# Two passages between stages and the start: where constants, first weights, the last turn and attention's rings stand

## The chip, the cores and the metric

One core of one Trainium2 chip runs the whole program. The metric is the device time of one execution, in microseconds (us). The core has five engines: TensorE (PE) for products, VectorE (DVE), ScalarE (ACT), GpSimd (POOL), and SyncE (SP), which here only issues transfers. Each runs its own list of instructions in order and waits on semaphores for the others.

## What is computed

Two layers on x of shape (4, 512, 512), in float32. Layer 0 attends from x to a context of 1601 rows per batch and gates the result; layer 1 is a transformer block whose products use one of two weight sets per token (`vm`). Cut to what the change touches:

```
memory_proj = memory @ W_mem.T                      # layer 0
attn = softmax(x @ memory_proj.T / sqrt(512))
memory_context = attn @ memory_proj
gate = sigmoid(concat([x, memory_context]) @ W_gate.T + b_gate)
x = rmsnorm(x + gate * memory_context, norm_w)

vm = (tt[:, :-1] == 1) & (tt[:, 1:] == 1)           # layer 1; the last token is False
mixed = where(vm, rmsnorm(x) @ v_qkv, rmsnorm(x) @ l_qkv)
q, k, v = split(mixed); q, k = rotary(q), rotary(k) # 16 heads of 32, tables by position_ids
x = x + where(vm, ctx @ v_dense, ctx @ l_dense)     # ctx = causal softmax(q k) v
... cross attention to the encoder rows, then a gated feed-forward, also by vm
```

## The kernel before, in words

The program is a row of stages, each a function with its own semaphores. A stage ends in `clear` (L71): a barrier of all engines, POOL clears the stage's semaphores, a second barrier. Within a stage each engine's list is written out by hand. The change touches the first three stages and the few lines that call them.

Nearly every product of two float32 operands is made of three (`three`, L106 to L108): each operand is split into a high part, a rounded copy, and a low part, the rest. The split of a weight tile, 128 x 512, loaded to the ring `w_raw` of 4, is a cast (high) and a subtraction (low).

**First stage, `gated_context` (L111).** A turn for each of the 4 batches. PE computes the maxima of rough scores (L443) in turn with the gate's share of x; DVE reduces them and makes `shift`; then come 13 key tiles, each with scores on PE, exponential on ACT (L251), a running sum on POOL and values on PE (L483). After the last tile DVE copies the values (L389), PE sums the columns (L524), DVE inverts (L391), PE spreads the inverse (L531), and the gate's second share follows. Between these short steps PE runs the four pieces of the next batch's first projection (`project`, L420), except in the last batch, where there is no next. The stream of batch b stays in `h` and is stored to `fused_d` by SP (L199, the last one L205).

Ahead of the first batch: SP loads x, W_mem, the context, the second half of W_gate and weight tiles, while ACT issues eight transfers of constants (L232, L236). DVE turns positions into a one-hot tile `hot`, which lies in `h`, copies masks and identities, then splits W_mem; PE multiplies the one-hot tile by the table (L490), which gives `cos_t` and `sin_t`, then runs the first `project` and the product of two weights for the gate (L498).

**Second stage, `queries_values_keys` (L559).** Again a turn per batch, batch 3 first, because its stream is still in `h`. A turn has three phases of 8 weight tiles: queries, values, keys (`part` 0, 1, 2; in each, 4 tiles of l_qkv, then 4 of v_qkv, masked by the rows of `keep_expert`). `find_keep` (L787) makes these rows out of the token types, and the flag `early_v` that tells PE which of two versions of the turn to run. DVE masks x (L823), ACT rounds it (L663), DVE makes the rest (L830); ACT squares the stream (L673), POOL adds the squares, PE sums them (`sums`, L944, two per turn, placed after the fourth tile). Queries and keys are turned: ACT copies the phase (L683), PE rotates (L936), POOL and DVE multiply and add, ACT and DVE split, and SP stores 8 pieces. The queries are rotated during the values' phase and the keys in the next turn's first phase; those of the last turn are rotated behind all products. In the first turn all 24 weight tiles are loaded, rounded on ACT (L655) and their rests made on DVE (L810). The stage ends with a store of `early_v` (L640), for which it waits.

**Third stage, `self_attention` (L999).** 16 groups of 4 heads. Rings of 4 groups (`k_r`, `q_r`, `v_r`) are filled by SP with 6 transfers for queries and keys and one for values per group, 256 KB each; `shifts` (L1050) stores a row of maxima and loads it back into the query ring. PE runs maxima for groups ahead between scores and values. The rings are buffers of this stage, so nothing is loaded before it begins.

## Time and profile before

| | us |
|---|---|
| median of 3 runs (lowest, highest) | 2306.26 (2303.32, 2311.72) |
| the profiled execution, device time | 2309.82 |
| its span | 2308.0 |
| PE busy | 2055.2 (89%) |
| VectorE busy | 1400.5 (61%) |
| ACT busy | 991.9 (43%) |
| POOL busy | 470.8 (20%) |
| first stage | 0 to 376 |
| second stage | 376 to 663 |
| self attention | 663 to 911 |

The profile is one execution; times in it count from the start of its span. The three runs spread over 8.4 us. The borders of the stages are the first transfers that SP issues in each. Rows of the timeline give start and duration in us; an idle time in brackets is the engine's own before that row, with what ended it. Matmuls are pipelined, so a matmul's duration is longer than its distance to the next.

### The profile page before, as it was taken

The page shows a single profiled execution, that of the slowest core. Times are in us where ns is not written, and L with a number is a line of the kernel's source. Part 1 is how long each engine was busy: PE and PEld are TensorE (multiplying, and loading weights), DVE is VectorE, ACT ScalarE, POOL GpSimd, SP SyncE. Part 2 cuts the span into 40 slices and gives each one's busy share as a digit, 9 for nine tenths or more (in the row PEclk, how much of TensorE's full clock was granted, in tenths as well). Part 3 has the DMA queues.
Part 4 walks back from the last instruction along what each step waited for, and adds up shares of the span by engine and source line. Part 5 has one row for each costly group of instructions (what it writes and reads, how often), then busy time and mean ns, then how long its engine had stood idle before and what let it go on. Part 6 is the DMA issues. An engine that isn't in the chain of part 4 may idle for free. (4 is left out here: it accounts for less than half of the span.)

```text
span 2308.0 us, 32376 instructions
## 1 busy us (share of the span) xinstructions
PE 2055.2 (89%) x12614; PEld 1343.3 (58%) x12614; DVE 1400.5 (61%) x1950; ACT 991.9 (43%) x1726; POOL 470.8 (20%) x483
## 2 busy tenths in 40 slices
PE   5999995899959996788849999999998799999878
PEld 3677674677745553676713444444434577878666
DVE  3344314666536774644578999999971565766444
ACT  1122313544414553444406888888885322221111
POOL 0211220233300111222200222222222112221111
PEclk9999997799969998889958999999999899999989
DMA  5122002433257662565472345435510433344232
GB/s 167 41 82 94 29 19 78 133 115 115 83 138 166 161 148 85 199 210 199 174 152 31 76 87 93 79 74 93 90 33 16 123 88 101 102 110 112 65 103 65
DMA packets 176917, 238.10 MB, mean 103 GB/s; under 512 B 26166, under 2 KB 105146, under 8 KB 174550
## 3 DMA queue, kind: packets, MB, share of 16 engines
q1 hardware_dynamic: 167352, 223.77, 36.2%
q0 software_dynamic: 7856, 10.90, 1.8%
q8 instruction: 116, 1.90, 0.4%
q10 hardware_dynamic: 1536, 1.07, 0.2%
q14 instruction: 57, 0.47, 0.1%
HBM read 169.61 MB, written 63.96 MB: 101 GB/s over the span
## 5 line engine op out<-in xcount | busy, mean ns | idle before, releaser
L1902 DVE TENSOR_REDUCE quarters<-ps 128x2 f32<-128x804 f32 x512 | 483.0, 992 | 51.8 <-PE ps L1936 49.9
L1867 ACT ACTIVATE pT_x<-ps 128x512 f32<-128x512 f32 (+1 forms) x832 | 451.5, 595 | 104.4 <-PE ps L1964 77.1
L1936 PE MATMUL ps<-kx_ring,qx_ring 63*128 63x402 f32 x1024 | 233.9, 469 | 38.1 <-DMA kx_ring<-cross_k_by_part 26.2
L1979 PE MATMUL ps<-pT_x,vx_ring 128*17 128x256 f32 (+1 forms) x3328 | 261.4, 387 | 0.2 <-ACT osb_x L1849 0.2
L1936 PEld LDWEIGHTS ps<-kx_ring,qx_ring 63*128 63x128 f32 x1024 | 100.3, 193 | 231.1 <-DVE quarters L1902 123.4
L106 PE MATMUL ps<-mi_h,w_hi 128*128 128x512 f32 (+1 forms) x440 | 175.1, 398 | 35.2 <-issue 23.7
L1964 PE MATMUL ps<-qx_ring,kx_ring 64*128 64x512 f32 (+1 forms) x832 | 174.8, 416 | 6.4 <-ACT pT_x L1867 2.6
L107 PE MATMUL ps<-mi_h,w_lo 128*128 128x512 f32 (+1 forms) x440 | 174.1, 396 | 0.0
L108 PE MATMUL ps<-mi_l,w_hi 128*128 128x512 f32 (+1 forms) x440 | 173.1, 393 | 0.0
L2120 POOL TENSOR_TENSOR sg<-sg,keep_all 128x512 f32<-128x512 f32 (+1 forms) x55 | 87.5, 1591 | 413.2 <-ACT sg L2099 413.2
L1134 DVE TENSOR_REDUCE row_max_s<-ps 128x1 f32<-128x384 f32 (+3 forms) x176 | 109.5, 633 | 70.6 <-PE ps L1166 69.8
L1110 ACT ACTIVATE pT_s<-ps 128x512 f32<-128x512 f32 (+1 forms) x176 | 96.0, 558 | 127.0 <-PE ps L1191 124.9
L100 DVE CAST w_hi<-w_raw 128x512 fp32r<-128x512 f32 (+1 forms) x165 | 83.3, 505 | 81.8 <-PE ps L108 61.3
L1979 PEld LDWEIGHTS ps<-pT_x,vx_ring 128*17 128x17 f32 (+1 forms) x3328 | 55.6, 95 | 110.9 <-issue 72.0
L102 DVE TENSOR_TENSOR w_lo<-w_raw,w_hi 128x512 fp32r<-128x512 f32 (+1 forms) x165 | 115.9, 702 | 5.7
L251 ACT ACTIVATE pT<-ps 128x512 f32<-128x512 f32 (+1 forms) x52 | 31.0, 597 | 203.7 <-PE ps L108 203.7
L106 PEld LDWEIGHTS ps<-mi_h,w_hi 128*128 128x128 f32 (+1 forms) x440 | 82.7, 188 | 56.1 <-issue 36.4
L2099 ACT ACTIVATE sg<-ps 128x512 f32<-128x512 f32 (+1 forms) x55 | 32.7, 595 | 190.6 <-PE ps L108 190.6
L2103 ACT ACTIVATE hid_h<-prod 128x512 fp32r<-128x512 f32 (+1 forms) x55 | 34.9, 634 | 177.1 <-DVE prod L2184 177.1
L483 PE MATMUL ps<-pT,cs 128*128 128x512 f32 (+1 forms) x208 | 97.1, 592 | 0.0
L1964 PEld LDWEIGHTS ps<-qx_ring,kx_ring 64*128 64x128 f32 (+1 forms) x832 | 77.1, 182 | 31.4 <-ACT pT_x L1867 27.6
L108 PEld LDWEIGHTS ps<-mi_l,w_hi 128*128 128x128 f32 (+1 forms) x440 | 82.6, 188 | 20.4
(310 smaller groups left out, 4341.5 us busy)
## 6 DMA issues: line engine op xcount, KB each, us to landing
kx_ring<-cross_k_by_part SPq DMA_DIRECT2D x96, 200.2 KB, 7.4
q_ring<-self_q_by_part SPq DMA_DIRECT2D x48, 256.0 KB, 4.3
k_ring<-self_k_by_part SPq DMA_DIRECT2D x48, 256.0 KB, 6.6
w_raw<-L_xattn_l_gate SPq DMA_DIRECT2D x40, 256.0 KB, 2.9
w_raw<-L_xattn_l_up SPq DMA_DIRECT2D x40, 256.0 KB, 2.9
w_raw<-L_xattn_l_down SPq DMA_DIRECT2D x40, 256.0 KB, 2.7
cross_v_by_group<-v_aug SPq DMA_DIRECT2D x16, 442.0 KB, 3.9
vx_ring<-cross_v_by_group SPq DMA_DIRECT2D x16, 442.0 KB, 10.2
```

The costliest lines, as they stand in the source:

```text
L102: nc.vector.tensor_tensor(out=lo, in0=raw, in1=hi.bitcast(f32), op=ALU.subtract).then_inc(s_split, 1)
L106: nc.tensor.matmul(dst, ah, bh, start=start, stop=False, **how)
L107: nc.tensor.matmul(dst, al, bh, start=False, stop=False, **how)
L108: return nc.tensor.matmul(dst, ah, bl, start=False, stop=stop, **how)
L483: last = nc.tensor.matmul(ps[:, other_bank(b, e), :], cs[0:kn, kt, e * P:(e + 1) * P], pT[0:kn, n % 3, :], start=kt == 0, stop=kt == KT - 1)
L1110: nc.scalar.activation(pT[:, u % 3, j:j + n, 0:width], heads_of(ps[:, SCORES + v % 3, :], n, width), ACT.Exp, scale=SCALE).then_inc(s["s_e ...
L1134: nc.vector.tensor_reduce(out=row_max[:, g % 2, j:j + heads, q], in_=heads_of(bank, heads, (q + 1) * P), axis=AX.X, op=ALU.max)\
L1867: nc.scalar.activation(pT[0:kn, u % 3, j, :], ps[0:kn, 5 + v % 3, :], ACT.Exp, scale=SCALE)\
L1902: nc.vector.tensor_reduce(out=quarters[:, g % 2, pair, :, q, quarter], in_=ps[:, at:at + 2, 0:MAXW], axis=AX.X, op=ALU.max)\
L1936: last = nc.tensor.matmul(ps[:, at + par, 0:MAXW], q_r[rows, g % RING, pair, q * P:(q + 1) * P], k_r[rows, g % RING, pair, k0:k0 + MAXW], ...
L1964: nc.tensor.matmul(ps[0:kn, 5 + (v + par) % 3, :], k_r[rows, g % RING, pair, k0:k0 + kn], q_r[rows, g % RING, pair, :], start=True, stop=T ...
L1979: last = nc.tensor.matmul(ps[j * HD:j * HD + CHD + 1, 4, queries], v_r[0:kn, g % RING, kt, j, :], pT[0:kn, u % 3, j, queries], start=kt == ...
```

## The change

**Start.** Of the eight constants ACT now loads two, `ident` and `cols`. SP loads W_mem ahead of x, and the half of W_gate ahead of the context. Everything made of the others (one-hot tile, tables, masks, `ident_b`) leaves the start.

**Last batch of the first stage.** The constants are loaded by SP, once the last context is split, into its free buffer `cT`, with the token types of batch 3. DVE, between `shift` and the copy of the values, splits four more weight tiles (l_qkv for the queries, tiles 0 to 3 of the second stage; they are loaded already in batch 0, behind the tiles of the gate) and then runs `constants_and_keep`: the position chain, the masks, and the keep rows and flag of batch 3. PE makes the two tables between the column sums' steps, ACT copies them. The stage no longer stores the last stream nor waits for that.

**Second stage.** It begins without `find_keep` and without the first four tiles. The stream of batch 3 is stored in the middle of the weights' loads. The last turn runs queries, keys, values, by `place`; its last two value pieces use `full`. SP loads attention's group 0 after the last queries are stored, and groups 1 and 2 with the row of ones after the last values, ahead of the store of `early_v`.

**Self attention.** Its rings lie in the second stage's weight buffers and in `w_raw`, held by the caller with nine semaphores, which are cleared in one more `clear` behind attention.

```diff
             tiles = [wgT_d[k * P:(k + 1) * P, :] for k in range(DT)] + [wmT_d[k * P:(k + 1) * P, :] for k in range(ET)]
+            tiles += [t["L1_xattn_l_qkv"][k * P:(k + 1) * P, 0:D] for k in range(DT)]
...
+                        sp.dma_start(wm, t["L0_xattn_W_mem"].rearrange("(a p) n -> p a n", p=P)).then_inc(s["s_wm"], 16)
                         load_x(0)
-                        sp.dma_start(wm, t["L0_xattn_W_mem"].rearrange("(a p) n -> p a n", p=P)).then_inc(s["s_wm"], 16)
+                        sp.dma_start(wg2[:, :, :], wgT_d[D:2 * D].rearrange("(a p) n -> p a n", p=P)).then_inc(s["s_wg2"], 16)
                         load_context(0)
-                        sp.dma_start(wg2[:, :, :], wgT_d[D:2 * D].rearrange("(a p) n -> p a n", p=P)).then_inc(s["s_wg2"], 16)
...
-                        sp.wait_ge(s["s_g"], 2 * DT * B)
-                        sp.dma_start(fused_d[B - 1], h[:, :, :]).then_inc(s["s_up"], 16)
-                        sp.wait_ge(s["s_up"], 16 * B)
+                        sp.wait_ge(s["s_tl"], NB * B)
+                        sp.dma_start(posi, t["pos_1xS"].broadcast_to((P, S))).then_inc(s["s_pos"], 16)
...
+                        sp.wait_ge(s["s_up"], 16 * (B - 1))
...
+                            if b == B - 1:
+                                for c, dst in enumerate((cos_t, sin_t)):
+                                    act.wait_ge(s["s_tab"], c + 1)
+                                    nc.scalar.activation(dst[:, :], ps[:, other_bank(b, 2 + c), :], ACT.Copy).then_inc(s["s_tabc"], 1)
...
                             if b + 1 < B:
                                 for k in range(DT):
                                     rest_x(b + 1, k)
+                            else:
+                                for n in range(DT + ET, len(tiles)):
+                                    split_tile(n)
+                                constants_and_keep()
...
+                        def table(c):
+
+                            pe.wait_ge(s["s_hot"], 4 + ST)
+                            pe.wait_ge(s["s_exp"], KT * B)
                             for a in range(ST):
-                                last = nc.tensor.matmul(ps[:, other_bank(0, 2 + c), :], tab[:, a, c, :], hot[:, a, :],
+                                last = nc.tensor.matmul(ps[:, other_bank(B - 1, 2 + c), :], tab[:, a, c, :], hot[:, a, :],
...
+        SELF_RING = 4
+
+        def self_group_loads(sp, g, k_r, q_r, v_r, s_key, s_value):
+
+            b, i, rows = g // (NH // 4), g % SELF_RING, slice(g % (NH // 4) * P, (g % (NH // 4) + 1) * P)
+            for ring, src, parts in ((q_r, qs_d, (0, 0, 1)), (k_r, ks_d, (0, 1, 0))):
+                for r, part in enumerate(parts):
+                    sp.dma_start(ring[r * HD:(r + 1) * HD, 4 * i:4 * i + 4, :].bitcast(f32),
+                                 src[b, part, rows, :].rearrange("(j d) n -> d j n", d=HD)).then_inc(s_key[i], 16)
+            sp.dma_start(v_r[:, i, :, :], vs_d[b, g % (NH // 4)]).then_inc(s_value[i], 16)
...
+                def place(i, part):
+
+                    return {0: 0, 1: 2, 2: 1}[part] if i == B - 1 else part
...
-                        load_tokens(0)
-                        for n in range(NT):
+                        for n in range(SPLIT, NT):
...
+                            if n == 2 * G:
+                                sp.dma_start(fused_d[turns[0]], h[:, :, :]).then_inc(s["s_hup"], 16)
...
+                            if i == B - 1:
+                                sp.wait_ge(s["s_wu"], done(i, 0))
...
+                                self_group_loads(sp, 0, k_r, q_r, v_r, s_key, s_value)
+                                for j in range(DT):
+                                    store_piece(2 * DT * i + DT + j)
...
-                        for j in range(DT):
-                            store_piece(2 * DT * (B - 1) + DT + j)
+                        sp.wait_ge(s["s_wu"], NT * B)
+                        sp.dma_start(k_r[3 * HD:3 * HD + 1, :, :].bitcast(f32).rearrange("a (r h) n -> a r (h n)", r=8),
+                                     ones_d[:, 0:SELF_RING * 4 // 8 * S].rearrange("(a r) n -> a r n", a=1)).then_inc(s_first, 16)
+                        for g in range(1, EARLY):
+                            self_group_loads(sp, g, k_r, q_r, v_r, s_key, s_value)
                         sp.dma_start(early_d.rearrange("b o n -> o (b n)"), early_v[:, :]).then_inc(s["s_eu"], 16)
...
-                            for n in range(3 * G):
+                            parts = (0, 2, 1) if i == B - 1 else (0, 1, 2)
+                            for m in range(3 * G):
+                                step, n = m % G, G * parts[m // G] + m % G
...
-                        for j in range(DT):
-                            rotate(B - 1, 1, j)
...
-        queries_values_keys()
-        self_attention()
+        both, first_sems = stage(names)
...
+            more_h, more_l = (sb(n, [P, 6 * DT - SPLIT, D], f32r, ctx=both) for n in ("qkv_h", "qkv_l"))
+            k_r, q_r = more_h[:, 0:4 * SELF_RING, :], more_l[:, 0:4 * SELF_RING, :]
+            v_r = w_raw[:, :, :].rearrange("p r (a n) -> p r a n", n=P)
+            queries_values_keys(more_h, more_l, k_r, q_r, v_r, s_kq, s_vr, s_first, EARLY)
+            self_attention(k_r, q_r, v_r, s_kq, s_vr, s_first, EARLY)
+            clear(first_sems)
```

TensorE at the end of the last batch: values (L483), column sums (L524) and the inverse's spread (L531) stood in a row before, ahead of the gate's share of the context.

```order
L108 MATMUL ps<-ul,ch 65x512
L483 MATMUL ps<-pT,cs 128x512 x4
L524 MATMUL ps<-ones,acc 128x1 x4
L531 MATMUL ps<-ident,rq 128x128 x4
L106 MATMUL ps<-cn_h,w_h 128x512
```

In the changed kernel (`cT` holds the table, `x_even` the one-hot tile):

```order
L517 MATMUL ps<-pT,cs 128x512 x4
L526 MATMUL ps<-x_even,cT 128x512 x4
L563 MATMUL ps<-ones,acc 128x1 x4
L526 MATMUL ps<-x_even,cT 128x512 x4
L572 MATMUL ps<-ident,rq 128x128 x4
L106 MATMUL ps<-cn_h,w_h 128x512
```

The two tables, made ahead of all else before, now stand on either side of the column sums.

SyncE's queue in the last turn, before: the last query piece's two stores, the value stores, the keys' stores (one of four pairs shown), the flags, and, behind the clearing, attention's first loads.

```order
L612 DMA self_q_by_part<-rows_h 128x512
L614 DMA self_q_by_part<-t 128x512
L636 DMA self_v_by_group<-v_nat 128x4x128 x4
L612 DMA self_k_by_part<-rows_h 128x512
L614 DMA self_k_by_part<-t 128x512
L640 DMA early_v_by_batch<-early_v 1x4
L591 UNCONDITIONAL_BRANCH
L1032 UNCONDITIONAL_BRANCH
L1041 DMA q_ring<-self_q_by_part 32x4x512 x3
L1041 DMA k_ring<-self_k_by_part 32x4x512 x3
```

The same in the changed kernel, where `qkv_l`, `qkv_h` and `w_raw` are attention's rings:

```order
L680 DMA self_q_by_part<-t 128x512
L607 DMA qkv_l<-self_q_by_part 32x4x512 x3
L607 DMA qkv_h<-self_k_by_part 32x4x512 x3
L609 DMA w_raw<-self_v_by_group 128x512
L678 DMA self_k_by_part<-rows_h 128x512
L715 DMA self_v_by_group<-v_nat 128x4x128 x2
L715 DMA self_v_by_group<-full_x 128x4x128 x2
L718 DMA qkv_h<-ones_rows 1x8x1024
L607 DMA qkv_l<-self_q_by_part 32x4x512 x3
L607 DMA qkv_h<-self_k_by_part 32x4x512 x3
L609 DMA w_raw<-self_v_by_group 128x512
L722 DMA early_v_by_batch<-early_v 1x4
```

Group 0's seven loads moved between the stores of queries and keys, the keys' stores ahead of the values', and the ones row with groups 1 and 2 (one of the two shown) ahead of the flags.

## Rows read from the trace of the kernel before

**Rows 1.** The page, busy time, share of the span and instructions by engine.

```profile
PE 2055.2 (89%) x12614; PEld 1343.3 (58%) x12614; DVE 1400.5 (61%) x1950; ACT 991.9 (43%) x1726; POOL 470.8 (20%) x483
```

**Rows 2.** Stretches: length; busy PE, PEld, DVE, ACT, POOL; PEclk, DMA share, GB/s.

```profile
10.00:20.00 10.00, 0.00 (x0) 0.00 (x0) 0.29 (x1) 1.32 (x3) 0.00 (x0) 1.00 1.05 389
100.00:140.00 40.00, 40.00 (x172) 30.24 (x171) 18.41 (x26) 12.13 (x17) 3.99 (x4) 1.00 0.32 106
665.00:670.00 5.00, 0.00 (x0) 0.00 (x0) 0.00 (x0) 0.00 (x0) 0.00 (x0) 0.50 1.05 229
672.00:697.00 25.00, 22.43 (x84) 14.87 (x88) 15.35 (x25) 3.71 (x7) 0.00 (x0) 0.50 0.88 186
675.00:680.00 5.00, 4.95 (x17) 2.70 (x15) 4.88 (x10) 0.00 (x0) 0.00 (x0) 0.50 1.06 189
```

**Rows 3.** Timeline, 0 to 66: start, duration, engine, line [idle before <-releaser].

```profile
9.13 2.19 ACT L216 ACTIVATE xh<-x_even 128x512 fp32r<-128x512 f32 x4 [1.82 <-DMA x_even<-x_transposed]
19.71 1.68 DVE L337 TENSOR_SCALAR h<-pT,tpos 128x512 f32<-128x512 f32 x4 [11.14 <-DMA acc<-c_masks]
30.25 0.80 PE L106 MATMUL ps<-xh,wm_h 128*128 128x512 f32 x1
47.11 3.02 PE L443 MATMUL ps<-ch,uh 128*128 128x402 f32 x8 [3.82 <-ACT ch L230]
```

**Rows 4.** DMA issues, 0 to 62 us: count, KB each, us to landing.

```profile
unscaled<-L_xattn_W_mem SPq DMA_DIRECT2D x1, 512.0 KB, 10.7
```

**Rows 5.** Timeline, batch 0: sixth tile's split, first rounding of the next x.

```profile
72.12 0.69 DVE L316 TENSOR_TENSOR wmT_l<-w_raw,wmT_h 128x512 fp32r<-128x512 f32 x1
82.07 0.62 ACT L216 ACTIVATE xh<-x_odd 128x512 fp32r<-128x512 f32 x1
```

**Rows 6.** Timeline, end of the last batch on VectorE and TensorE.

```profile
349.68 1.29 DVE L389 COPY unscaled<-ps 128x512 f32<-128x512 f32 x2 [43.93 <-PE ps L483]
355.68 0.79 PE L106 MATMUL ps<-cn_h,w_h 128*128 128x512 f32 x1 [2.17 <-DVE cn_l L401]
359.69 0.63 PE L106 MATMUL ps<-cn_h,w_h 128*128 128x512 f32 x1
```

**Rows 7.** Timeline, 370 to 410 us: second stage, first turn.

```profile
370.87 0.33 SPq L205 DMA_DIRECT2D stream_after_gate<-h  x1
383.10 1.41 DVE L823 SCALAR_TENSOR_TENSOR full_x<-h,w_both,keep_expert 128x512 f32<-128x512 f32 x2
396.93 1.13 ACT L673 ACTIVATE sq<-h 128x512 f32<-128x512 f32 x2
408.77 2.08 PE L944 MATMUL ps<-sq,ones 128*128 128x512 f32 x2 [4.74 <-POOL sq L762]
```

**Rows 8.** Timeline, 646 to 673 us: the passage to attention.

```profile
646.62 2.06 ACT L683 ACTIVATE plain<-ps 128x512 f32<-128x512 f32 x4 [11.55 <-PE ps L108]
659.66 0.32 SPq L640 DMA_DIRECT2D early_v_by_batch<-early_v  x1
663.11 1.28 SPq L1041 DMA_DIRECT2D q_ring<-self_q_by_part  x3
672.35 0.61 PE L1163 MATMUL ps<-mask_qk,ident_b 128*128 128x512 bf16 x1 [21.38 <-DMA k_ring<-self_k_by_part]
```

**Rows 9.** Attention: timeline 693 to 705; a shift's landing; the groups' sums.

```profile
693.50 0.59 PE L1163 MATMUL ps<-mask_qk,ident_b 128*128 128x512 bf16 x1 [1.34 <-DMA k_ring<-self_k_by_part]
697.50 0.31 SPq L1053 DMA_DIRECT2D shift_by_head<-shift_s  x1
703.11 0.23 SPq L1056 DMA_DIRECT2D q_ring<-shift_by_head  x1
704.72 0.23 PE L1188 MATMUL ps<-mask_kq,ident_b 128*128 128x128 bf16 x1 [0.70 <-DMA q_ring<-shift_by_head]
...
shift_by_head<-shift_s SPq DMA_DIRECT2D x3, 8.0 KB, 1.4
...
L1101 ACT ACTIVATE osb_s<-ps x16: 1023/1024/1024, 708.7 to 902.4; 128x1024 f32<-128x1024 f32 x16
```

More of the change, by code:

```diff
@@ L520, in _ @@
                                 project(b + 1, 0)
+                            else:
+                                table(0)
                             pe.wait_ge(s["s_un"], ET * (b + 1))
@@ L528, in _ @@
                                 project(b + 1, 1)
+                            else:
+                                table(1)
                             pe.wait_ge(s["s_rq"], b + 1)
@@ L585, in queries_values_keys, with value_tile, done @@
                 any_early, rs_col = sb("any_early", [1, 1], ctx=ctx), sb("rs_col", [P, ST], ctx=ctx)
+                def value_tile(i, a):
+                    return full[:, a - 2, :] if i == B - 1 and a >= 2 else v_nat[:, a % 2, :]
+                def place(i, part):
+                    return {0: 0, 1: 2, 2: 1}[part] if i == B - 1 else part
+                def done(i, part):
+                    return NT * i + G * (place(i, part) + 1)
                 def split_of(n):
@@ L676, in keep_plain @@
                         def keep_plain(i, group):
-                            act.wait_ge(s["s_wu"], NT * i + (3 * G if group else G))
+                            act.wait_ge(s["s_wu"], done(i, 2 * group))
                             for j in range(DT):
@@ L712, in keep_values @@
                                 o = ST * i + a
-                                if o >= 2:
+                                if o >= 2 and not (i == B - 1 and a >= 2):
                                     act.wait_ge(s_uv[a % 2], 16 * (o // 2))
-                                nc.scalar.activation(v_nat[:, a % 2, :], ps[:, bank(3 * i + 1, a), :], ACT.Copy, scale=rs_col[:, a:a + 1])\
+                                nc.scalar.activation(value_tile(i, a), ps[:, bank(3 * i + place(i, 1), a), :], ACT.Copy,
+                                                     scale=rs_col[:, a:a + 1])\
                                     .then_inc(s["s_vn"], 1)
@@ L741, in _ @@
                                 round_piece(2 * DT * i + j)
+                            if i == B - 1:
+                                keep_plain(i, 1)
+                                for j in range(DT):
+                                    round_piece(2 * DT * i + DT + j)
                             keep_values(i)
@@ L787, in find_keep @@
                         def find_keep(i):
-                            kp, first = keeps[i % 2], NK * i
-                            dve.wait_ge(s["s_tt"], 16 * (i + 1))
+                            kp, first = keeps[i % 2], NK * (i - 1)
+                            dve.wait_ge(s["s_tt"], 16 * i)
                             if i >= 2:
@@ L935, in rotate @@
                             pe.wait_ge(s["s_pl"], o + 1)
-                            nc.tensor.matmul(ps[:, bank(3 * i + 2 * group, j), :], rot[:, :], plain[:, j, :], start=True, stop=True)\
+                            nc.tensor.matmul(ps[:, bank(3 * i + place(i, 2 * group), j), :], rot[:, :], plain[:, j, :], start=True, stop=True)\
                                 .then_inc(s["s_rot"], 1)
@@ L955, in run @@
                                     sums(i, 0)
                                     sums(i, 1)
[L957 to L959 removed]
+                                if m // G == 1 and step < 2:
+                                    rotate(i, 0, 2 * step)
+                                    rotate(i, 0, 2 * step + 1)
+                                if i == B - 1 and m // G == 2 and step < 2:
+                                    rotate(i, 1, 2 * step)
+                                    rotate(i, 1, 2 * step + 1)
@@ L974, in _ @@
                                 run(i, S - P)
-                        for j in range(DT):
-                            rotate(B - 1, 1, j)
                 clear(sems)
@@ L1005, in self_attention @@
             s = dict(zip(names.split(), sems))
-            s_kq, s_vr = ([s[f"{n}{i}"] for i in range(RING)] for n in ("s_kq", "s_v"))
+            s["s_one"] = s_first
             GB, SCALE = NH // 4, float(HD) ** -0.5
@@ L2250, in program @@
         gated_context()
-        queries_values_keys()
-        self_attention()
+        names = "s_kq0 s_kq1 s_kq2 s_kq3 s_v0 s_v1 s_v2 s_v3 s_one"
+        both, first_sems = stage(names)
+        s_kq, s_vr, s_first = first_sems[0:4], first_sems[4:8], first_sems[8]
+        with both:
+            EARLY = 3
+            more_h, more_l = (sb(n, [P, 6 * DT - SPLIT, D], f32r, ctx=both) for n in ("qkv_h", "qkv_l"))
[4 more added lines that the diff above has]
+            clear(first_sems)
         projections(dense)
```

230 lines of the change are left out of this document (121 added, 109 removed).

## The prediction

> **What bounds the kernel now.** I read the shares first: TensorE (PE) is busy 89% of a span of 2308.0 us, the next engine, VectorE (DVE), 61% [rows 1]. So time can be won only where PE stands still or runs at its low clock. The stretches tell where: inside the batches it is busy 40.00 of 40 us at granted clock 1.00, but at 10 to 20 and at 665 to 670 us it does nothing, and at 675 to 680 it is busy 4.95 of 5 us and still at 0.50, the lower of its two levels (1.2 of 2.4 GHz) [rows 2]. The change touches three places: the start, the passage from the first stage to the second, and that from the second to attention. The stages behind are untouched, but for one more clearing of semaphores.
>
> The sum is made against the profiled execution, 2309.8 us, 3.6 us over the median of the shown runs (2306.3); I take the difference off the median.
>
> **1. The start (gain 18.2 us).** DVE waits 11.14 us for the masks, the last of the constants, until 19.71; only then do one-hot tile, position tables and, at 30.25, PE's first projection of x follow. Yet x had landed at 9.13, where ACT rounds it [rows 3]. The change takes positions, table and masks (0.9 MB) out of the opening transfers and puts W_mem (0.5 MB) ahead of x. At the 389 GB/s of 10 to 20 us [rows 2] 0.5 MB takes 1.3 us; x has 0.5 MB more ahead of it on its queue and 0.9 MB less beside it, so I put it at 8.5 us, W_mem earlier. A rounding and a rest (1.3 us) later PE starts, at 9.8, 20.4 us earlier. It starts at the low clock, whose price the last batch shows: 2.2 us (part 2). The rest of the chain, to the first maxima at 47.11 [rows 3], keeps its length, so these start at 28.9. The context, now fourth, has 4.3 MB in and ahead of it: 11 us at that rate, landed by 16 or 17, and wanted at 25. The weights are behind it and wanted later still. Bounds: W_mem, issued at 1.3 behind x, landed 10.7 us later [rows 4]; if x lands only when both had, at 12.0, PE is 3.5 us later and the gain 14.7; if x lands 2 us earlier than I say, it is 20.2.
>
> Not free but covered: SP now loads four query tiles before x of batch 1, and the last of these waits for the split of the sixth tile, which ends at 72.8 in old time. ACT rounds that x at 82.07 [rows 5]; 1 MB landed within 8.4 us even in the crowded opening (0.75 to 9.13). With that cover gone, batch 0 would slip by the excess.
>
> **2. Last batch (gain 1.0 us).** DVE gets four tile splits (4.4 us), positions and one-hots (3.7), masks (1.3) and keep rows (2.3), together some 12 us, by the durations that these steps had where they stood. They lie in the 43.93 us in which DVE waits for the values [rows 6]. Their seven transfers are issued once batch 2 is stored, some 15 us before anyone needs them. PE gets the two tables, 4 products of 0.43 us each, where the earlier batches have projections. The first fills the gap before the sums; the second stands in front of the reciprocal's broadcast and delays it by 1.2 us. But in these gaps PE's clock had fallen: its products from 355.68 on, after a wait of 2.17, were slow (0.63 us a row, the last such at 359.69) until 360.3 [rows 6], and half of these 4.6 us was lost, 2.2 us. With the gaps filled and only the one of 2.1 us left, I expect the clock to hold. Bounds: +1.0, and -1.2 if it falls all the same.
>
> **3. First to second stage (gain 12.3 us).** Before, SP stores the stream at 370.87, waits for it, and the stage is cleared; tokens are loaded, DVE makes the keep rows, and the first masked x is at 383.10 [rows 7]. What clearing costs alone: the early flags are written at 659.66 and the next stage's first issue is 3.45 us later [rows 8]; such a small write takes 1.4 us [rows 9], so 2.1 us. The masked x moves to 373.1, 10.0 us earlier. PE's own start is not what counts: it waits for the sums of squares, whose first step is at 396.93, after the eighth rounding, and whose second sum is at 408.77 [rows 7]. From 383.10 to 396.93 there are eight tiles of 1.7 us; for four of them DVE no longer makes a weight's rest (0.6 us): 2.3 us. Together 12.3, and the turn's later steps hang on that sum. The store of the stream moves in among the weights' loads (1 MB, 2.7 us of queue) and delays loads whose rounding starts 9 us later. Bounds: 10.0, if tiles 4 to 7, loaded only after the clearing, hold DVE up; 13.5, if all eight are quicker.
>
> **4. Second stage to attention (loss 0.3 us).** The largest rearrangement, and I give it nothing. Before: PE's products of the last turn end where ACT takes them, 646.6; the keys are turned, the flags written at 659.66, the first load issued at 663.11, and PE resumes at 672.35 after waiting 21.38 us [rows 8]. In the new order keys go second, and their turning (12.5 us) lies beside the values (some 16.8 us). PE ends at 648.4, since four rotations (1.75 us) are now inside. The values are copied and their stores issued by 651.6. Next on SP, though, stand the ones row and two groups' loads (14 of 256 KB, 3.67 MB), and only behind them the early flags, for which the stage's end waits. Loads of this shape moved 229 and 189 GB/s [rows 2]: with the middle of 225 15.8 us, and 1.8 us to start, from 652.3 to 669.9. That a small write waits for loads issued ahead of it is seen in attention: the shift's usual 1.4 us became 5.61 (697.50 to 703.11) [rows 9] behind two groups. So the flags return at 670.5, clearing ends at 672.6, and PE starts there: 0.3 late. Bounds: +10.0, if the write is not held (out at 659.1, back at 660.4, PE at 662.4); -3.9 at 189 GB/s throughout.
>
> The Trainium skill (DMA: Bandwidth & Descriptors, Queues, rings and completion order) says that completion is not in order per issuing engine and that a small transfer may use few of the 16 engines. By that the flags need only their own engine's share of the loads done; with even shares that is the same 670.5, with uneven ones somewhat less. No row separates these.
>
> **5. Attention's start (gain 2.0 us).** Groups 0 to 2 are resident, so PE's waits of 1.34 us at 693.50 and 0.70 us at 704.72 [rows 9] go, and group 3 meets empty queues. Late next are DVE's maxima, as before. I take the clock as it is now, 0.50 over the first 25 us, 672 to 697 [rows 2].
>
> The Trainium skill (TensorE: Matmul & The Clock Gate, Part 1: The HAM clock gate) says that the array is throttled after idling and released by sustained activity. The stretch of 675 to 680, full and still low, does not bear that out here. By the page the clock would be up early in attention and the sum 7 us better: the second rival.
>
> **6. The extra clearing** behind attention costs at most the 2.1 us of part 3; I take 2.0 lost.
>
> Sum: 18.2 + 1.0 + 12.3 - 0.3 + 2.0 - 2.0 = 31.2 us. 2306.3 - 31.2 = 2275.
>
> **The rivals.**
> - *The small write is not held* (10%). Part 4 then gives its 10.0: gain 41.5, 2265. For it: 16 bytes are no load. Against: the 5.61 us.
> - *The clock rises early in attention* (7%). PE is busy 22.43 of 25 us there [rows 2]; at full clock it would save up to half of the 20 us after 677, but DVE's maxima then bind, so some 7 us. Gain 38.2, 2268. Against: 4.95 of 5 us busy did not do it.
> - *Each part at its low end* (12%): x late (3.5), clock falls in part 2 (2.2), late tiles (2.3), loads at 189 GB/s (3.6): gain 19.6, 2287.
> - *The clock stays low in attention* (4%), the one that ends slower. A group there takes (902.4 - 708.7) / 15 = 12.9 us [rows 9] at full clock, with PE full, and as much again at half. Before, the clock rose only after PE had stood still at 693.50 and then run on; without that stall nothing in the trace says when it rises. Two such groups eat up 26 us, three all of it; four make 2275 + 52 = 2327. Against: in the batches and in the second stage it rose within some 6 us of dense products. Half of the 4% goes to two or three groups (no change), half to four and more.
> - That the moved query weights bring nothing, or the loads nothing, is in the cases above: the start alone is 14.7 us or more.
>
> **How the numbers follow.** The forecast has 67%. 0.5% is 11.5 us, about what a measurement of this kernel can tell from no change; all cases but the last (96%) are faster by more. The range 2262 to 2287 takes in both fast rivals and the forecast's own bounds, and leaves out the low-clock case and the half of the low-end case that goes beyond 2287.
>
> **What would show it.** The first maxima start at 27 to 31 us. No stretch at 0.50 follows the last batch's reciprocal. The second sum of squares comes 31.5 us before 408.77. Between the last value product of the last turn and attention's first product lie 24 us, with the flags' write in flight for some 10. If PE resumes within 16 us, part 4 is wrong; if the maxima begin after 33, part 1 is; if the clock is at 0.50 beyond 30 us after attention's start, the slow rival holds.

## The result

| | us |
|---|---|
| before, median of 4 runs (lowest, highest) | 2304.79 (2301.09, 2311.72) |
| changed, median of 4 runs (lowest, highest) | 2341.88 (2337.68, 2342.79) |
| changed over before, 95% interval | 1.0154 (1.0126 to 1.0182) |
| forecast | 2275 (2262 to 2287), chance of slower 2% |

The change makes the kernel 37 us slower; I had it 31 us faster. The profiled execution (2342.79 us, span 2341.0) shows both a gain and a larger loss. The page's first part:

```profile
PE 2071.2 (88%) x12597; PEld 1345.2 (57%) x12614; DVE 1402.5 (60%) x1952; ACT 991.6 (42%) x1724; POOL 472.5 (20%) x483
```

Against [rows 1] PE is busy 16 us longer for the same products: more of its work ran at the lower clock. The timeline at the start, at the end of the last batch and in the second stage's first turn:

```profile
8.13 2.19 ACT L226 ACTIVATE xh<-x_even 128x512 fp32r<-128x512 f32 x4 [5.17 <-DMA x_even<-x_transposed]
9.63 0.76 PE L106 MATMUL ps<-xh,wm_h 128*128 128x512 f32 x1 [9.63 <-DVE xl L304]
27.65 3.02 PE L477 MATMUL ps<-ch,uh 128*128 128x402 f32 x8 [3.82 <-ACT ch L240]
...
329.80 3.60 PE L526 MATMUL ps<-x_even,cT 128*128 128x512 f32 x8
334.05 3.68 PE L526 MATMUL ps<-x_even,cT 128*128 128x512 f32 x8
340.79 0.50 PE L106 MATMUL ps<-cn_h,w_h 128*128 128x512 f32 x1 [2.17 <-DVE cn_l L435]
...
355.05 1.42 DVE L907 SCALAR_TENSOR_TENSOR full_x<-h,w_both,keep_expert 128x512 f32<-128x512 f32 x2 [1.27 <-PEq L76]
363.56 0.80 PE L106 MATMUL ps<-xe0h,w_hi 128*128 128x512 f32 x1 [11.31 <-DVE xe1l L914]
366.97 1.14 ACT L755 ACTIVATE sq<-h 128x512 f32<-128x512 f32 x2
378.93 1.12 PE L1032 MATMUL ps<-sq,ones 128*128 128x512 f32 x2 [1.10 <-POOL sq L847]
```

The first maxima come 19.46 us earlier (47.11 to 27.65), the combined products 14.89 (355.68 to 340.79), the masked x 28.05, the second sum of squares 29.84. Then the passage to attention:

```profile
620.83 0.80 SPq L718 DMA_DIRECT2D qkv_h<-ones_rows  x1
...
628.12 0.43 SPq L609 DMA_DIRECT2D w_raw<-self_v_by_group  x1
628.60 0.29 SPq L722 DMA_DIRECT2D early_v_by_batch<-early_v  x1
...
641.95 1.31 PE L1238 MATMUL ps<-qkv_h,qkv_l 96*128 96x128 f32 x4 [24.22 <-PEq L76]
```

PE resumes 30.40 us earlier than before, at 641.95 instead of 672.35. So far all is as forecast. The sums of the groups in attention then start 31.8 us earlier and end 34.5 us later than [rows 9] (708.7 to 902.4):

```profile
L1173 ACT ACTIVATE osb_s<-ps x16: 1024/1024/1026, 676.9 to 936.9; 128x1024 f32<-128x1024 f32 x16
```

A group takes (936.9 - 676.9) / 15 = 17.3 us on average instead of 12.9: attention lost 66.3 us. The stretch 680 to 865, then one group of it in pieces of 5 us (columns as in [rows 2]):

```profile
680.00:865.00 185.00, 152.29 (x1147) 83.47 (x1152) 98.97 (x156) 66.78 (x115) 18.58 (x20) 0.86 0.48 113
...
742.00:747.00 5.00, 2.19 (x23) 0.93 (x21) 2.21 (x5) 0.76 (x2) 1.84 (x2) 0.97 0.53 144
747.00:752.00 5.00, 4.26 (x24) 1.99 (x24) 1.25 (x2) 1.19 (x2) 0.00 (x0) 0.50 0.00 2
752.00:757.00 5.00, 5.00 (x43) 3.12 (x40) 2.64 (x4) 2.80 (x5) 0.00 (x0) 0.84 0.33 88
```

Before, PE was busy 191.84 of 193 us in the like stretch (709 to 902), at granted clock 1.00. Now it stands still once a group and runs slow behind that. The waits say for what: TensorE's from 655 to 950, and the SP queue's own from 680 to 865 (total, times, longest):

```profile
PE ps L1260 <- DMA qkv_l<-shift_by_head: 37.7, 12, 3.6
...
SPq L1128 <- PE ps L1285: 73.6, 9, 9.0
SPq L1137 <- DMA shift_by_head<-shift_s: 59.8, 10, 6.6
```

Twelve waits, all for the shift: the row of maxima that DVE makes, that goes out to DRAM (8 KB) and comes back into the queries' ring. They are those of groups 2 to 13, whose shifts stand in SP's list behind the loads of groups 4 to 15. The last two shifts, with no load ahead, are back in 1.41 and 1.34 us (908.52 to 909.93, 920.24 to 921.58), and PE does not wait for them. The timeline of SP and TensorE for one group:

```profile
734.73 1.27 SPq L607 DMA_DIRECT2D qkv_l<-self_q_by_part  x3
736.04 1.38 SPq L607 DMA_DIRECT2D qkv_h<-self_k_by_part  x3
737.47 0.44 SPq L609 DMA_DIRECT2D w_raw<-self_v_by_group  x1
739.14 0.31 SPq L1134 DMA_DIRECT2D shift_by_head<-shift_s  x1
745.55 0.23 SPq L1137 DMA_DIRECT2D qkv_l<-shift_by_head  x1
...
747.74 0.29 PE L1260 MATMUL ps<-mask_kq,ident_b 128*128 128x128 bf16 x1 [3.54 <-DMA qkv_l<-shift_by_head]
```

Seven loads (1.8 MB) are issued, 1.2 us later the shift's write, and this small write takes 6.4 us until its read can be issued. In the kernel before the same four steps stand differently:

```profile
743.33 1.27 SPq L1041 DMA_DIRECT2D q_ring<-self_q_by_part  x3
744.64 1.38 SPq L1041 DMA_DIRECT2D k_ring<-self_k_by_part  x3
748.93 0.34 SPq L1048 DMA_DIRECT2D v_ring<-self_v_by_group  x1
753.38 0.31 SPq L1053 DMA_DIRECT2D shift_by_head<-shift_s  x1
754.84 0.23 SPq L1056 DMA_DIRECT2D q_ring<-shift_by_head  x1
```

The keys' and queries' six loads leave 5.6 us ahead of the value's and 10.1 us ahead of the shift, and the write takes 1.5 us. In the diff that is one helper. Before, the six loads waited for the scores of group g - 4 (s_sc) and only the value's load for its value products (s_pv); `load_group` waits for both ahead of all seven. I had read past this line.

### The profile page after: what moved, and what is told of

The parts are those of the page before. It is cut to its first block and busy times, and to the rows that moved or that the text cites. A ratio compares the mean times of both kernels' runs of the same rounds, so it can differ in the third digit from the quotient of the medians.

```text
span 2341.0 us, 32399 instructions
## 1 busy us (share of the span) xinstructions
PE 2071.2 (88%) x12597; PEld 1345.2 (57%) x12614; DVE 1402.5 (60%) x1952; ACT 991.6 (42%) x1724; POOL 472.5 (20%) x483
## 3 DMA queue, kind: packets, MB, share of 16 engines
q1 hardware_dynamic: 168600, 224.76, 35.8%
## 5 line engine op out<-in xcount | busy, mean ns | idle before, releaser
L1238 PE MATMUL ps<-qkv_h,qkv_l 96*128 96x128 f32 (+3 forms) x256 | 98.1, 444 | 24.2 <-PEq L76 24.2
```

Of the source, the lines that this page charges most:

```text
L1238: last = nc.tensor.matmul(bank[:, m * width:(m + 1) * width], q_r[0:STACK, at + m, cut], k_r[0:STACK, at + m, 0:width], start=False, stop= ...
```

## The experiments

Theory A: the joined wait is the whole loss, and the rest of the change brings what was forecast. Rival B: the rings in the weights' buffers, the resident groups or the clock at attention's start (the slow rival of the prediction) carry it. Every ratio below is to the kernel before as timed beside that variant. Its medians were 2310.87 us (two waits, the joined wait alone, shift first, flags first), 2308.3 (late groups, old turn order, second table), 2306.06 (all together, tokens first) and 2307.56 (shift through ACT's queue).

**Two waits again**, in the changed kernel.

```diff
                             if g >= RING:
                                 sp.wait_ge(s["s_sc"], NU * (g - RING + 1))
+                            self_key_loads(sp, g, k_r, q_r, s_kq)
+                            if g >= RING:
                                 sp.wait_ge(s["s_pv"], ST * (g - RING + 1))
-                            self_group_loads(sp, g, k_r, q_r, v_r, s_kq, s_vr)
+                            sp.dma_start(v_r[:, g % RING, :, :], vs_d[g // GB, g % GB]).then_inc(s_vr[g % RING], 16)
```

> The changed kernel, but attention's loads wait as before: a group's six query and key transfers for the scores of the group four back, only its value transfer for that group's values. Theory A (the joined wait is the whole loss in attention: loads issued some 5.6 us later keep the shift's small write in the queue for 6 us, PE waits 3 us a group and its clock falls): attention takes 233 us as before instead of 300, clock 1.00 in its body, in all 2275 us. Theory B (the rings' new place, in the weights' buffers and w_raw, makes attention slow): stays near 2342. Theory C (the clock stays low by itself, as in the prediction's slow rival, because the start of attention lacks a stall): clock under 0.9 and above 2310 although no wait for the shift is left.

Measured: 2277.96 us, ratio to before 0.9863 (0.9847 to 0.9879). Attention's sums, and then the stretch 680 to 865:

```profile
L1180 ACT ACTIVATE osb_s<-ps x16: 1024/1024/1024, 677.1 to 870.8; 128x1024 f32<-128x1024 f32 x16
```

```profile
680.00:865.00 185.00, 183.84 (x1654) 105.72 (x1657) 137.05 (x214) 97.54 (x169) 26.14 (x28) 1.00 0.54 132
```

12.9 us a group, as before, no wait for the shift, full clock. Undoing one joined wait makes the changed kernel 64 us faster (67 by the ratios, 1.0154 to 0.9863) and puts it within 3 us of my forecast. The rest of the change is worth 1.4%, 31.6 of 2304.79 us.

**The joined wait alone**, in the kernel before.

```diff
                             if g >= RING:
                                 sp.wait_ge(s["s_sc"], NU * (g - RING + 1))
+                                sp.wait_ge(s["s_pv"], ST * (g - RING + 1))
...
-                            if g >= RING:
-                                sp.wait_ge(s["s_pv"], ST * (g - RING + 1))
                             sp.dma_start(v_r[:, g % RING, :, :], vs_d[g // GB, g % GB]).then_inc(s_vr[g % RING], 16)
```

> The kernel before with nothing but the joined wait: the six query and key transfers also wait for the values of the group four back. Theory A: slower by about 65 us, 2370, with PE waiting some 3 us a group for the shift's row. Theories B and C: no change, 2305.

Measured: 2373.54 us, ratio 1.0282 (1.0254 to 1.0309), 63 us slower; the sums run from 707.6 to 964.2 (17.1 us a group), and from 700 to 860 TensorE waits

```profile
PE ps L1187 <- DMA q_ring<-shift_by_head: 26.3, 8, 3.9
```

The same loss with the old rings and nothing resident: the rings and the early groups have no part in it.

**The shift ahead of the loads**, the joined wait kept.

```diff
+                            shifts(g)
                             if g + 2 < NG and g + 2 >= EARLY:
                                 load_group(g + 2)
-                            shifts(g)
```

> The changed kernel with its joined wait, but in each turn of the queue the shift's write and read stand ahead of the next group's loads instead of behind them. Theory A in its narrow form (only the small write behind seven big loads costs): the write is back in 1.4 us, 2275 to 2285 us. If the loads being late costs by itself: PE waits for the key ring and it is between 2285 and 2340. Theory B: near 2342.

Measured: 2299.8 us, ratio 0.9952 (0.9936 to 0.9968). The timeline of one group on SP, and then TensorE's wait from 700 to 860:

```profile
722.29 0.31 SPq L1134 DMA_DIRECT2D shift_by_head<-shift_s  x1
723.64 0.23 SPq L1137 DMA_DIRECT2D qkv_l<-shift_by_head  x1
723.98 1.26 SPq L607 DMA_DIRECT2D qkv_l<-self_q_by_part  x3
```

```profile
PE ps L1235 <- DMA qkv_h<-self_k_by_part: 10.2, 8, 1.9
```

With nothing ahead of it the write takes 1.35 us, and 42 of the 64 us are back. What is left is a new wait: loads issued later still come late for the maxima of their group, 1.3 us at a time (sums 675.6 to 886.6, 14.1 us a group). So the narrow form of the theory (2275 to 2285) was wrong: the joined wait costs by the late loads too.

**The shift through ACT's queue**, all else as in the changed kernel.

```diff
+                            if g + 1 < NG and i == 5:
+                                act.wait_ge(s["s_used"], place["turn", g + 1] + 1)
+                                act.dma_start(shift_d[(g + 1) % 2], shift[:, (g + 1) % 2, :].bitcast(f32)).then_inc(s["s_so"], 16)
+                            if g + 1 < NG and i == 8:
+                                act.wait_ge(s["s_so"], 16 * (g + 2))
...
```

> The changed kernel with its joined wait and its order on SP kept; only the shifts of groups 1 to 15 are written and read back through ACT's queue instead of SP's (the write behind ACT's sixth exponential of the group before, the read behind its ninth, some 3.5 us later). If the write is held because it stands behind seven loads in one queue, it now lands in 1.3 to 3 us, PE's waits for the shift (37.7 us) and the low clock behind them go, and the time falls to 2280 to 2300 us (2278 is that of separate waits; the loads are still late by the joined wait). The rival, that 1.8 MB under way hold any small write, whatever its queue, expects it to land in 5 us or more, ACT to wait for it, and 2335 us or more.

Measured: 2339.96 us, ratio 1.0138 (1.0121 to 1.0155), like the changed kernel. The issues from 680 to 865 (count, KB each, median us to landing), then the timeline of one group on ACT, then TensorE's waits from 655 to 950:

```profile
shift_by_head<-shift_s ACTq DMA_DIRECT2D x10, 8.0 KB, 6.4
```

```profile
741.42 0.31 ACTq L1187 DMA_DIRECT2D shift_by_head<-shift_s  x1
747.93 0.23 ACTq L1191 DMA_DIRECT2D qkv_l<-shift_by_head  x1
```

```profile
PE ps L1267 <- DMA qkv_l<-shift_by_head: 35.2, 12, 3.6
```

I expected the queue to be the cause, and was wrong: here SP issued the seven loads at 737.01 to 740.16, the write went out by another queue, and took 6.5 us all the same. ACT's queue by itself is not slow: the writes of the last two groups, with no load under way, landed in 1.4 us (median). So what holds the write is the loads under way, not the place behind them in one queue. Behind this write ACT's own list stood still too (12 waits, 48.5 us), which the rival had expected; the time of this variant is therefore no price of the queue alone.

**The flags first**: two waits, and the early flags' store ahead of the ones row and the loads of groups 1 and 2.

```diff
+                        sp.dma_start(early_d.rearrange("b o n -> o (b n)"), early_v[:, :]).then_inc(s["s_eu"], 16)
                         sp.wait_ge(s["s_wu"], NT * B)
...
                         for g in range(1, EARLY):
                             self_group_loads(sp, g, k_r, q_r, v_r, s_key, s_value)
-                        sp.dma_start(early_d.rearrange("b o n -> o (b n)"), early_v[:, :]).then_inc(s["s_eu"], 16)
```

> x1 with the write of the early flags issued ahead of the ones row and the loads of groups 1 and 2 at the end of the second stage. By part 4 of the prediction the flags then return while the values' stores end, clearing ends some 10 us earlier and PE resumes about 14 us after its last value product instead of 24: 10 us faster than x1, 2265. Rival: PE or the shift's row then waits for the loads of group 1 that are still under way, and half or more of it is given back: 2270 or more.

Measured: 2272.7 us, ratio 0.983 (0.9814 to 0.9846).

```profile
623.06 0.81 SPq L722 DMA_DIRECT2D early_v_by_batch<-early_v  x1
...
630.84 0.43 SPq L614 DMA_DIRECT2D w_raw<-self_v_by_group  x1
632.92 0.58 PE L1242 MATMUL ps<-mask_qk,ident_b 128*128 128x512 bf16 x1 [12.96 <-PEq L76]
```

PE resumes 10.0 us earlier than with the flags behind the loads (642.92), the +10.0 of part 4's upper bound; its idle time falls from 23.79 to 12.96. Of these the median shows 5, on the rival's side of its border (2270 or more). But the rival's cause isn't there: between 633 and 860 PE waits for no load and no shift, and in the two profiles attention ends 10.1 us apart. In the stage behind it the three batches after the first take 57.3, 54.5 and 58.4 us with the flags behind and 60.7, 58.4 and 57.3 with the flags first, for the same program: 6 us more. With late groups, where the flags go first too, the three take 170.7 us together, like the 170.2 with the flags behind; so that stage varies by some 6 us from one execution to the next. Now SP's own issues end the passage: the last is out at 631.27, and PE starts 1.65 us later.

**Groups 1 and 2 loaded in attention**, the flags first: the early loop is dropped, and attention's SP begins with `load_group(1)`, `shifts(0)`, `load_group(2)`.

> The variant with two waits and flags first, with the loads of groups 1 and 2 back in attention, as before (group 1 ahead of the first shift, group 2 behind it); group 0 stays early. If SP's 14 issues (6.6 us, 624.66 to 631.27) end the stage, PE resumes about 5 us earlier than 632.92 (before, the first issue of attention came 3.45 us behind the flags' issue), and the time falls to 2267 to 2270 us. The rival, that the early loads of groups 1 and 2 are what lets PE run on into group 1 without a wait, expects PE to wait for keys of group 1 by some 5 us and 2273 us or more.

Measured: 2263.23 us, ratio 0.982 (0.9799 to 0.984).

```profile
625.18 0.78 SPq L722 DMA_DIRECT2D early_v_by_batch<-early_v  x1
...
629.53 1.31 PE L1247 MATMUL ps<-qkv_h,qkv_l 96*128 96x128 f32 x4 [7.45 <-PEq L76]
...
638.76 0.59 PE L1244 MATMUL ps<-mask_qk,ident_b 128*128 128x512 bf16 x1 [0.22 <-DMA qkv_h<-self_k_by_part]
```

The idle time falls from 12.96 to 7.45 us, as expected; PE's resume is only 3.4 us earlier, because the last product ended 2.1 us later in this profile. Group 1 makes PE wait 0.22 us and group 2 0.80 us (650.36). The two medians are 9 us apart, but their kernels before differ too: the ratios are only 0.1% apart, within both intervals. So no difference of the whole time is shown, only one on the path up to attention. From the first product to the first sums it is 35.8 us here (629.53 to 665.3) against 34.0 with the groups resident (632.92 to 666.9): residence gives back 1.8 of the 5.5 us that its issues cost.

**The last turn in its old order** (queries, values, keys), else as with the flags first: `parts = (0, 1, 2)` for all turns, the keys' turn and its rotations and stores behind the values.

> The variant with two waits and flags first, with the last turn's parts back in the order queries, values, keys (the keys' turn and its four rotations at the end, as before); group 0's loads stay early. What the new order is worth: before, the flags were written 13.1 us after the last product (646.59 to 659.66), now 3.1 us (619.98 to 623.06). My theory expects PE to resume 10 us later than the 632.92 of the variant it is compared with (about 643), and 2278 to 2283 us. The rival, that loads and the clearing of semaphores set the passage whichever part ends the turn, as the step of my prediction on this passage had it (24 us either way), expects PE to resume within 3 us of 633 and no change of the time.

Measured: 2273.74 us, ratio 0.9853 (0.9834 to 0.9872).

```profile
643.54 1.31 PE L1242 MATMUL ps<-qkv_h,qkv_l 96*128 96x128 f32 x4 [17.38 <-PEq L76]
```

PE resumes 10.6 us later than with the new order, as expected. Of these 1.75 us were there before the last turn (second sum of squares at 380.84 instead of 379.09, with the same code up to it), so the new order is worth some 9 us up to attention once the flags are not held. The change as it stands resumes at 641.95 and this variant at 643.54: the hold of its flags ate the new order up. The whole time is under the 2278 to 2283 that I expected: the ratios differ by 0.23%, with intervals that overlap, a gain of some 5 us, not firmly shown.

**The second table behind the spread**, and one clearing instead of two: the four products of `table(1)` follow the reciprocal's broadcast, ACT copies sin_t behind cn_h; the nine shared semaphores are cleared with attention's own.

> On top of the variant with two waits and flags first: the second table's four float32 products (3.43 us on PE in the last batch) stand behind the inverse's spread instead of ahead of it, so that 2.17 us of them fill the idle time before the combined products, and the nine shared semaphores are cleared with the attention's own. My theory expects the last batch's products 2.2 us earlier, attention's store to the next stage 0.7 us shorter, and 2.9 us off the time (about 2270). The rival, that DVE's and ACT's chain behind the spread is held by the table (its copy to sin_t on ACT behind cn_h), expects no gain.

Measured: 2261.99 us, ratio 0.9807 (0.9789 to 0.9826).

```profile
334.47 1.16 PE L572 MATMUL ps<-ident,rq 128*128 128x128 f32 x8 [0.27 <-DVE rq L427]
335.46 3.60 PE L528 MATMUL ps<-x_even,cT 128*128 128x512 f32 x8
338.50 0.80 PE L106 MATMUL ps<-cn_h,w_h 128*128 128x512 f32 x1
```

The combined products start 2.5 us earlier (340.96 to 338.50), and the second sum of squares 2.15. From attention's last store to the next stage's first transfer it is 3.8 us instead of 4.2, 0.4 us less where I expected 0.7. The ratio falls by 0.23%, some 5 us where I expected 2.9, with intervals that overlap: the gain is shown on the path, not in the whole time.

**All of them together**: two waits, flags first, late groups, second table behind the spread, one clearing.

> Two waits, flags first, second table behind the spread, one clearing, and groups 1 and 2 loaded in attention: the edits of four variants together. If their gains add, PE resumes about 2.2 us before the 629.53 of the variant with late groups (627), attention's store to the next stage stays at 3.8 us, and the median lies at 2256 to 2261 us. The rival, that what is gained before attention is given back in the stage behind it (its four batches took 50.6 + 57 to 61 us each, and not the same in any two profiles), expects 2261 to 2264 us, no better than either variant alone.

Measured: 2260.25 us, ratio 0.9802 (0.9775 to 0.9829). PE's combined products start at 338.38, as with the later table, and its idle time ahead of attention is 7.46 us, as with the late groups: on these two passages the edits add. PE resumes at 624.30 (expected 627); the other 3 us come from neither passage. Attention's last store goes out at 859.15. The median is at the border of the two accounts, and 1.7 us from the variant with the second table: over the whole kernel it isn't shown that the edits add. It is the fastest median of all versions, 46 us ahead of the kernel before and 82 of the changed one.

**The tokens first again**, one execution only, on the version above.

> The same with the first four loads back in the order of before (tokens, W_mem, context, gate weights), everything else of the start as changed. W_mem then lands where the tokens land now (about 8.1 us instead of 4.4), DVE's split of it (1.9 us) stands behind that and ahead of the tokens' rests. My theory expects PE's first product at 11 us instead of 9.6 and all behind it 1.3 us later; so the order of the loads is 1 to 2 us of the 19.5 us gained at the start, and the moved constants are the rest. The rival, that the order of the loads carries the start, expects 5 us or more.

Measured: 2260.25 us, too little to compare the whole time; only the start is read.

```profile
7.90 0.69 DVE L377 CAST wm_h<-unscaled 128x1024 fp32r<-128x1024 f32 x1 [5.07 <-DMA unscaled<-L_xattn_W_mem]
...
10.60 0.76 PE L106 MATMUL ps<-xh,wm_h 128*128 128x512 f32 x1 [10.60 <-DVE xl L306]
```

PE's first product is 0.8 us later (9.79 to 10.60), the first maxima 0.86 (27.62 to 28.48). The order of the loads is about 1 us of the 19.5 (expected 1.3), far from the rival's 5 or more. The first maxima vary by more than that in unchanged starts (last section), the first product by less (9.43 to 9.79). The rest of the 19.5 us is put down to the moved constants by subtraction.

## Why the prediction was wrong

The sign was wrong through one step of part 5: "group 3 meets empty queues. Late next are DVE's maxima, as before". That was argued for groups 0 to 3 alone. The loads of groups 4 to 15 stand in the sum at nothing, without a reason; I did not ask what the new helper does to them. It held their query and key loads for the value products as well, and the shift's write of groups 2 to 13 went out behind 1.8 MB of loads and came back after some 6.4 us instead of 1.5. Two things that I had in hand would have told it: the diff, with two waits before one call, and [rows 9], where I read that a write behind two groups' loads took 5.61 us and used it for the flags of part 4. The same small write stands in every group, and moving 1.6 MB of loads 5.6 us closer to it makes it late twelve times. The price: 37.7 us of waits, and 28.6 us for the low clock behind them, together the 66.3. The second term is seen by itself too: from the first sums to the last PE is busy 221.12 us, against 192.53 before, with the same products.

That the low clock comes with the stall is in the windows of one group: PE busy 2.19 of 5 us, then a granted clock of 0.50 for 5 us and 0.84 for the next. The Trainium skill (TensorE: Matmul & The Clock Gate, Part 1: The HAM clock gate) has idling throttle the array; here the trace agrees, group for group. The slow rival of the prediction, that the clock stays low through attention, named a loss of this size (2327) for another reason and is not what happened: the clock rises 26 us behind attention's first product (641.95 to 668), as in the kernel before (672.35 to 698), and then falls with each stall and recovers in each group. So the prediction's sign for that rival, a clock of 0.50 beyond 30 us, would have pointed at the wrong cause (0.50 from 690 to 695).

The other parts, by the profiles of the changed kernel and of the one with two waits (us, gains positive):

| part | forecast | measured |
|---|---|---|
| 1 start | +18.2 | +19.5: x at 8.13 (forecast 8.5), PE at 9.63 (9.8) |
| 2 last batch | +1.0 | -2.4 up to the last x of the batch |
| 3 first to second stage | +12.3 | +12.8 |
| 4 second stage to attention | -0.3 | +0.6: resume 30.40 earlier, 29.84 of it from parts 1 to 3 |
| 5 attention's start | +2.0 | +2.2 with two waits (first sums 31.6 earlier, resume 29.4) |
| 5 loads of groups 4 to 15, not seen | 0 | -66.3 |
| 6 the extra clearing | -2.0 | -0.7 (3.24 to 3.92 us from attention's store to the next issue) |

That the parts other than the missed one add up to the forecast within 1 us is in part luck: part 2 came out 3.4 us lower, the others together 4.2 higher.

Part 2 was mis-sized. I priced a table at 4 products of 0.43 us; the row of the old tables had shown sixteen records for eight products. Each float32 product of 512 columns is two records of 0.43 us, and a table 3.44 us (329.80 to 333.24). From the last value product to the combined products it is therefore 5.0 us longer than before (10.99 us instead of 6.03), where I had 1.2. What I said of the clock held in this profile: no slow product follows the 2.17 us gap, where before they lasted until 360.3, and the 2.2 us came back (12.29 us from there to the last x instead of 14.47). It doesn't hold always: in the profile of the old turn order, with the same code and the same gap, the products are slow until 344.7. The last x of the batch (h) ends at 353.08 instead of 370.15, 17.07 earlier, of 19.46.

Part 3 came out by its own terms: the masked x 28.05 earlier, 11.0 more than the end of the stage before (forecast 10.0), and the tiles 1.9 (forecast 2.3).

Part 4 was right in its mechanism: 24 us from the last value product to the resume (24.22), because the flags' write is held. PE came 13.35 us behind the issue of the flags (628.60 to 641.95), against 4.35 where no loads are ahead of them (625.18 to 629.53). That the size agrees to 0.2 us is partly luck. The sum has two slips: the middle of 229 and 189 GB/s is 209, not 225, and 3.67 MB take 16.3 us at 225, not 15.8; from 631 to 637 the loads moved 227 GB/s. The bound of +10.0 for an unheld write was met when the store was moved (10.0). But the reason that I gave, the place behind the loads in the queue, is open to doubt after the run through ACT's queue; for the flags' own write no other queue was tried.

## What to carry to other kernels

When two waits are joined into one helper, write down for each transfer behind it when it could leave before and when now, and what small, latency-bound transfer goes out next; a few kilobytes that the main engine waits for should leave before the bulk loads, or long enough behind them. Loads that are made resident early cost their issue time at the border of a stage (0.47 us each here), so count that against the wait they remove. And if a step in one place rests on a row, look for every other place in the loop to which the same row applies.

## What the runs showed of the hardware

- **A small write is held by loads under way, in another queue too.** 8 KB took 1.35 us with nothing ahead, 6.4 us when issued 1.2 us behind 1.8 MB from the same queue, and 6.4 us (median of ten) through ACT's queue with the loads on SP's, where it took 1.4 with no load under way. The Trainium skill (DMA: Bandwidth & Descriptors, Queues, rings and completion order) says two things here: that each engine takes turns between the queues for which it has work, and that the write which raises a transfer's semaphore lands only after every earlier write of that engine, across its queues. By the first alone I'd expect the write to get through early; the second fits the 6.4 us. So does a third account, that the write waits on DMA engines that are full (DMA share 1.06 from 737 to 742). No run here tells them apart.
- **The clock rises at different times in the same program.** PE's first products run at the low clock until 13.28 us in the profile of the changed kernel, until 15.94 with two waits, though the program's start is the same and the first product comes at 9.63 and 9.66. The first maxima come at 27.65 and 28.89; over all profiles with this start they lie between 27.38 (shift through ACT's queue) and 28.89. After the 2.17 us gap at the end of the last batch it was at full in six profiles of the same code and fell in one (341.20, old turn order).
- **Full and still slow.** At attention's start PE is busy 6.00 of 6 us at 0.50 (631 to 637, with late groups), and 24.12 of 25 us (642 to 667, changed kernel), and the clock rises only some 24 to 27 us behind the first product, in the kernel before as with its 1.34 us stall gone (two waits). Later in attention, behind a stall of 3.4 to 3.6 us, it is back 4 to 7 us after the stall's end (733 behind 729.13, 716 behind 709.22). Nothing here separates the two; it stays open.
- **PE starts the second stage late.** Its first product is at 363.56, behind 11.31 us of idleness, although the operands that it needs were ready at 357.2. PE still waits 1.10 us for the second sum of squares at 378.93, so an earlier start would gain nothing up to there; it was not followed up.
